# Masked graph attention with eight heads: the output projection takes two heads in one matmul, from data that DMAs move

## The chip, the cores and the metric

The kernel runs on one core of a Trainium2 chip. A core has TensorE (PE, matmuls; its weight loads are told apart as PEld), VectorE (DVE), ScalarE (ACT), GpSimd (POOL) and SyncE (SP), which issues the DMAs here. The metric is the time of one execution on the device in microseconds.

## The reference

Eight graphs (b) of 1024 nodes with 64 features each; adj is an integer matrix of 1024 x 1024 per graph in which about 8 of 1024 entries of a row are not zero. All in float32:

```
h = max(layernorm(x), 0)
q, k, v = h @ Wq + bq, h @ Wk + bk, h @ Wv + bv          # 8 heads of 64
scores = leaky_relu(q . k / 8 + edge_bias[adj], 0.2)     # per head, 1024 x 1024
attn = softmax(where(adj > 0, scores, -1e9))
x + (attn @ v, heads side by side) @ Wp + bp
```

## The kernel before

**Folded weights.** The start folds the weights: scores come from h and a product of Wq and Wk, and v and Wp are folded per head into a 64 x 64 block W_h, so that the output is the sum over heads of (attention-weighted h) @ W_h. These blocks lie in w_ext, [128, 8, 65]: rows 0 to 63 hold W_h, and row 64 has a one in column 64.

**Sparse keys.** The rows of a graph are cut into 8 tiles of 128 queries, and each tile into 8 groups of 16 queries. For each group the kernel gathers the keys that at least one of its queries is joined to, at most 32 from each block of 128 nodes, 256 slots in all. The eight heads of 16 queries are 128 rows, so scores of a group are 128 x 256. A second branch of the program (dense_programs) serves inputs that break these limits; it doesn't run here.

**Steps.** All engines run the same sequence of steps written out in Python. Step s does pair p = s - SCORE of the scores, while other stages work at other lags of the table at line 43 ff.: a stage of lag L treats pair s - L. A pair is two groups; a tile is 4 pairs, so 4 steps; a graph is 32 steps, and there are 32 + 256 steps. `tile(b, s, L)` is true once per tile, `piece(b, s, L, n)` in n steps per tile. Each engine does its share of a step in a fixed order, and semaphores tie them.

A tile runs through: adj_in loaded (LOAD, SP), made bf16 (CONV, POOL), transposed (TURN_A, PE, then ACT), counted (COUNT, PE), ranked, one-hot matrices made (mark, DVE L1670), the masks gathered (MASK, PE L1199, copied to mask_own by ACT L1423), the keys gathered (TFILL, PE L1187, ACT L1432). Then per pair: scores (PE L1164 and L1165, float32r), take_scores (DVE L1658, adds the mask and takes the maximum), the leaky line (POOL L1034), their maximum (DVE L1681), transposes (turn_y, PE L1175), exp (ACT L1441), weigh (PE L1222: probabilities times h and a column of ones, so that row 64 of its result is the sum of the probabilities), copy_o (ACT L1449) to ot_sb, [65, 2, 8, 128], by tile parity.

**Masks.** The masks are made with 16 queries x 8 groups in the rows, but the scores want each query's mask in 8 rows, one per head. move_masks (SP, lag MASK_OUT = 14) stores a tile's masks in DRAM (one DMA of 512 KB), waits until it has landed, and reads them back eight times (mask_rows, eight DMAs of 64 KB). take_scores of that tile's first pair (lag 17) waits for all eight.

**The end of a tile.** project (PE L1253, lags PROJ = 27 and 28) runs twice per tile, with e = 0 and 1, for four heads each: one float32 matmul per head with ot_sb[0:65] of the head as weights (128 columns) and w_ext[0:65] streamed (65 columns), into adj_bank. Column 64 of each result is the sum of the probabilities. A float32 matmul shows in the trace as two pairs of LDWEIGHTS and MATMUL. norm (DVE, lags NORM = 28 and 29) clamps the sums, takes reciprocals, and multiplies; in its first call it also adds the mean of v to rows without any neighbour (`alone`). add_heads (POOL, SUM = 30) adds the eight heads and the residual. SP stores four tiles at once (OUT = 31) and then loads the rows of x for the next graph (x_res). adj_bank is shared with turn_adj and count (PE), whose waits `free` works out: turn_adj (s mod 4 = 1) follows project's second call (s mod 4 = 0) and waits for norm's product of it.

**SP's queue.** SP executes its waits and DMA issues in program order: in a step load_adj, load_stack, move_masks, load_natural, the store of the output. In the start-up, store_graph(k), which stores two forms of a graph's h in DRAM, comes after the steps 0, 2, ... up to 14.

**w_sum** (DVE, s = 18) is the sum of W_h over heads, in both halves of the rows; one matmul per graph (L1329) multiplies the mean of h with it.

## Time and profile before

| what | value |
|---|---|
| median of 3 runs | 1035.78 us (1034.2 to 1037.22) |
| the profiled execution's own time | 1032.86 us |
| its span, first to last instruction | 1030.6 us |
| PE busy | 95% of the span |
| PEld busy | 94% |
| DVE busy | 89% |
| ACT busy | 75% |
| POOL busy | 47% |
| DMA | 125.20 MB in 190760 packets, q1 40.9% of 16 engines |

The busy shares are of the whole span, start-up and end included. A PE matmul's duration is the time from its start to its modelled end, and neighbours overlap, so the cost of one is the distance to the next. "Idle before" is time in which an engine did nothing just before an instruction, with what ended it; "issue" means nothing that the profile shows.

### The profile page before, as it was taken

To read this page: it belongs to the slowest core of one execution; us is meant where nothing else is said; L and a number is where in the kernel's file an instruction comes from. 1 tells how busy PE (TensorE), PEld (TensorE's weight loads), DVE (VectorE), ACT (ScalarE), POOL (GpSimd) and SP (SyncE) were. 2 spreads that over 40 slices of the span, in tenths; PEclk is the share of its full clock that TensorE was granted. 3 is DMA by queue.
4 is the path that set the end of the run, shared out by engine and by line. 5 is a ranking of instruction groups with operands and counts; after the bars stand their busy time and mean duration, and the time that the engine had idled before them with its cause. 6 is when DMAs were issued, how large, how long until landed. Compare 5 with 4: busy or idle time off the path is not lost.

```text
span 1030.6 us, 28703 instructions
## 1 busy us (share of the span) xinstructions
PE 978.6 (95%) x9056; PEld 965.4 (94%) x9056; DVE 914.2 (89%) x3409; ACT 776.0 (75%) x1737; POOL 487.2 (47%) x865
## 2 busy tenths in 40 slices
PE   4578999999999999999999999999999999999996
PEld 4468999999999999999999999999999999999995
DVE  3878899889998999898998899989998899989984
ACT  3587787788778787887777777878777887788762
POOL 1004455455545454554554455545454545555454
PEclk9989999999999999999999999999999999999998
DMA  7574534344343444434343343435343344433220
GB/s 175 184 227 122 145 107 131 104 114 136 113 133 114 121 127 116 134 104 143 103 130 108 113 145 101 137 103 151 104 137 103 109 132 121 135 113 109 77 70 9
DMA packets 190760, 125.20 MB, mean 121 GB/s; under 512 B 32832, under 2 KB 180300, under 8 KB 190604
## 3 DMA queue, kind: packets, MB, share of 16 engines
q1 hardware_dynamic: 189812, 122.75, 40.9%
q8 instruction: 78, 1.28, 0.5%
q10 hardware_dynamic: 792, 0.53, 0.3%
q14 instruction: 78, 0.64, 0.2%
HBM read 79.19 MB, written 44.04 MB: 120 GB/s over the span
## 4 chain that ended last, share of the span: by engine, by line
PE 84%; DVE 9%; issue 2%; DMA 1%; ACT 1%; POOL 1%; SPq 0%; ACTq 0%; POOLq 0%; DVEq 0%
PE bank L1222 20%; PE bank L1253 11%; PE bank L1175 10%; PE bank L1210 8%; PE bank L1164 6%; PE bank L1312 6%; PE bank L1165 5%; PE bank L1187 5%; PE bank L1199 5%; PE bank L1230 3%; DVE w L1658 2%; PE bank L1238 1%; DVE w L1681 1%; DVE o_all L1757 1%; PE bank L1298 1%
## 5 line engine op out<-in xcount | busy, mean ns | idle before, releaser
L1034 POOL TENSOR_SCALAR a_line<-w,a_bias 128x256 f32<-128x256 f32 x512 | 263.3, 514 | 453.3 <-DVE w L1681 411.3
L1222 PE MATMUL bank<-pt,nat_sb 128*65 128x128 f32 x2048 | 265.4, 273 | 0.2
L1658 DVE CUSTOM_DVE_ANT_0 w<-bank,mask_rows 128x256 f32<-128x256 f32 x512 | 195.9, 418 | 60.9 <-issue 56.8
L1441 ACT ACTIVATE pt<-bank 128x512 f32<-128x512 f32 x256 | 153.9, 601 | 110.9 <-PE bank L1175 105.9
L1681 DVE SCALAR_TENSOR_TENSOR w<-w,shift,a_line 128x256 f32<-128x256 f32 x512 | 229.9, 488 | 2.5 <-POOL a_line L1034 2.5
L1222 PEld LDWEIGHTS bank<-pt,nat_sb 128*65 128x65 f32 x2048 | 230.7, 138 | 0.6 <-issue 0.6
L1670 DVE TENSOR_TENSOR onehot<-val,counts_to 128x512 fp32r<-128x512 f32 x256 | 181.1, 707 | 2.2
L1423 ACT ACTIVATE mask_own<-bank,mask_bias 128x512 bf16<-128x512 f32 x256 | 175.1, 684 | 1.1 <-PE bank L1199 1.1
L1175 PE MATMUL bank<-ident,w 128*128 128x128 f32 x1024 | 154.0, 273 | 0.0
L1432 ACT ACTIVATE t_sb<-bank 128x512 fp32r<-128x512 f32 x256 | 150.2, 587 | 2.7 <-PE bank L1187 2.6
L1164 PE MATMUL bank<-t_sb,q_hi 128*128 128x256 f32 x512 | 142.8, 301 | 1.1 <-DVE wmax L1658 1.0
L1253 PE MATMUL bank<-w_ext,ot_sb 65*128 65x65 f32 x1024 | 138.9, 279 | 3.8 <-DVE o_all L1757 3.0
L1449 ACT ACTIVATE ot_sb<-bank 65x256 f32<-65x256 f32 x256 | 97.9, 383 | 55.7 <-PE bank L1222 55.7
L1210 PEld LDWEIGHTS bank<-both_halves,t_sb 128*128 128x128 f32 x1024 | 136.5, 191 | 0.0
L1210 PE MATMUL bank<-both_halves,t_sb 128*128 128x64 f32 x1024 | 136.0, 256 | 0.0
L1468 ACT ACTIVATE q_hi<-bank,q_bias 128x256 fp32r<-128x256 f32 x256 | 107.5, 476 | 36.0 <-PE bank L1312 36.0
L1165 PE MATMUL bank<-t_sb,q_lo 128*128 128x256 f32 x512 | 133.6, 283 | 0.0
L1022 POOL TENSOR_TENSOR o_all<-o_all 128x256 f32<-128x256 f32 (+2 forms) x192 | 120.8, 629 | 21.6 <-DVE o_all L1757 6.6
L1253 PEld LDWEIGHTS bank<-w_ext,ot_sb 65*128 65x128 f32 x1024 | 124.8, 192 | 4.6 <-issue 2.9
L1187 PE MATMUL bank<-onehot,h_nl 128*128 128x256 f32 x512 | 124.1, 324 | 0.4 <-ACT t_sb L1432 0.4
L1632 DVE SCALAR_TENSOR_TENSOR q_lo<-bank,q_bias,q_hi 128x256 fp32r<-128x256 f32 x256 | 111.3, 475 | 9.1 <-ACT q_hi L1468 6.0
L1175 PEld LDWEIGHTS bank<-ident,w 128*128 128x128 f32 x1024 | 118.9, 141 | 0.1
(135 smaller groups left out, 1619.5 us busy)
## 6 DMA issues: line engine op xcount, KB each, us to landing
adj_in<-in_adj_dram SPq DMA_DIRECT2D x64, 512.0 KB, 4.0
mask_store<-mask_own SPq DMA_DIRECT2D x64, 512.0 KB, 3.5
mask_rows<-mask_store SPq DMA_DIRECT2D x512, 64.0 KB, 2.4
nl_store<-nl_ring SPq DMA_DIRECT2D x7, 512.0 KB, 4.1
stack_store<-stage SPq DMA_DIRECT2D x7, 512.0 KB, 2.9
h_stack<-stack_store SPq DMA_DIRECT2D x7, 512.0 KB, 4.5
h_nl<-nl_store SPq DMA_DIRECT2D x28, 128.0 KB, 3.6
x_res<-in_x_dram SPq DMA_DIRECT2D x16, 128.0 KB, 2.3
```

Source lines behind the costliest of these rows:

```text
L1034: nc.gpsimd.tensor_scalar(a_line[:, i % 2, :], w[:, i, :], 5.0, a_bias[:, i:i + 1], ALU.mult, ALU.add)\
L1164: pe.matmul(dst, q_hi[:, y % 2, GPT * (t % 2) + g, :], keys, start=True, stop=False)
L1165: last = pe.matmul(dst, q_lo[:, y % 2, GPT * (t % 2) + g, :], keys, start=False, stop=True)
L1175: last = pe.transpose(turned_bank[:, P * (2 * u + k):P * (2 * u + k) + P], w[:, slot(p, u), P * k:P * k + P], ident[:, :])
L1187: last = pe.matmul(t_bank[:, 256 * i:256 * i + 256], h_nl[:, 2 * f + i, :], onehot[:, t % 2, 2 * f + i].rearrange("p g j -> p (g j)"), sta ...
L1210: last = pe.matmul(nat_bank[:, D * (2 * u + k):D * (2 * u + k) + D], keys[:, P * k:P * k + P], both_halves[:, :], start=True, stop=True)
L1222: last = pe.matmul(o_part[0:D + 1, P * u:P * u + P], nat_sb[:, t % 2, p % 4 * 2 + u, k, :], pt[:, p % 2, u, k, :], start=(k == 0), stop=(k ...
L1253: last = pe.matmul(adj_bank[:, (D + 1) * h:(D + 1) * h + D + 1], ot_sb[0:D + 1, t % 2, 4 * e + h, :], w_ext[0:D + 1, 4 * e + h, :], start= ...
L1423: nc.scalar.activation(mask_own[:, t % 2].rearrange("p g t j -> p t g j")[:, 2 * f:2 * f + 2], m_bank[:, :].rearrange("p (t g j) -> p t g ...
L1658: nc.vector.tensor_tensor_reduce(w[:, i, :], row_bank[:, SLOTS * u:SLOTS * u + SLOTS], mask_rows[:, t % 2, p % 4 * 2 + u, :], 0.25, LEAST_ ...
L1670: nc.vector.tensor_tensor(onehot[:, t % 2, 2 * f:2 * f + 2].rearrange("p t g j -> p (t g) j"), val[:, t % 2, cols * f:cols * f + cols].uns ...
L1681: nc.vector.scalar_tensor_tensor(w[:, i, :], w[:, i, :], shift[:, i:i + 1], a_line[:, i % 2, :], ALU.add, ALU.max).then_inc(y_ready, 1)
```

## The change

- project takes two heads at once. w_pair, [128, 4, 128], holds for heads 2c and 2c + 1 their blocks W on the diagonal: rows 0 to 63 and columns 0 to 63 for the first, the other halves for the second, zeros elsewhere. o_pairs, [128, 2, 4, 128], holds the two heads' results one under the other. A call issues two float32 matmuls of 128 rows, 128 columns of weights and 128 columns streamed.
- The second head of a pair has to move from rows 0 to 63 to rows 64 to 127. move_o on SP (lag MOVE_O = 26) does this with one DMA for each of the two halves (64 rows, 4 pieces of 512 B each), and a third one brings row 64, the sums of 8 heads, into 8 rows (den_rows). Project's first call of a tile turns these with one more float32 matmul (8 rows of weights, 128 columns, against the 8 x 8 identity).
- norm's first call clamps and inverts all eight sums, its second only multiplies. `summed` is waited for just before x_res is written.
- PROJ, NORM, SUM and OUT go from 27, 28, 30, 31 to 31, 32, 34, 35.
- move_masks is split: store_masks in step lag 14, behind move_o in SP's order, spread_masks in step lag 15.
- w_sum has two halves of rows from the two diagonal blocks, and the matmul with the mean of h adds them (two matmuls).
- count and convert get one wait more each (adj_ready, a_turned). COUNT and TURN_A keep their lags 6 and 5.

```diff
-    SCORE, A_LINE, Y, TURN, PV, X_ADD, PROJ, NORM, SUM, OUT = 17, 19, 20, 21, 22, 24, 27, 28, 30, 31
+    MASK, MASK_OUT, MASK_IN, TFILL, QFILL, BETA, COLSUM, VEC = 10, 14, 15, 13, 9, 6, 18, 22
+    SCORE, A_LINE, Y, TURN, PV, X_ADD, MOVE_O, PROJ, NORM, SUM, OUT = 17, 19, 20, 21, 22, 24, 26, 31, 32, 34, 35
...
-            def move_masks(b, t):
+            def store_masks(b, t):
...
                 sp.dma_start(whole, mask_own[:, par].rearrange("p g t j -> p g (t j)")).then_inc(mask_stored[par], 16)
+
+            def spread_masks(b, t):
+
...
                 sp.wait_ge(mask_stored[par], 16 * before + 16)
                 for h in range(H):
                     sp.dma_start(mask_rows[GQ * h:GQ * h + GQ, par], own).then_inc(mask_in[par], 16)
+
+            def move_o(b, t):
+
+                n, par = TPG * b + t, t % 2
+                sp.wait_ge(o_copied, 4 * n + 4)
+                if later(n, 2):
+                    sp.wait_ge(proj_done, 2 * n - 2)
+                heads = o_turned[0:D, par].rearrange("p (c a) q -> p c a q", a=2)
+                for a, rows in enumerate((slice(0, D), slice(D, P))):
+                    sp.dma_start(o_pairs[rows, par], heads[:, :, a]).then_inc(o_moved[par], 16)
+                sp.dma_start(den_rows[0:H, par], o_turned[D:D + 1, par]).then_inc(o_moved[par], 16)
...
+                t = tile(b, s, MOVE_O)
+                if t is not None:
+                    move_o(b, t)
                 t = tile(b, s, MASK_OUT)
                 if t is not None:
-                    move_masks(b, t)
+                    store_masks(b, t)
+                t = tile(b, s, MASK_IN)
+                if t is not None:
+                    spread_masks(b, t)
...
             def project(b, t, e, s):
                 n = TPG * b + t
-                pe.wait_ge(o_copied, 4 * n + 4)
-                free(adj_bank_uses, b, s, len(list(adj_bank_uses(b, s))) - 1)
-                for h in range(4):
-                    last = pe.matmul(adj_bank[:, (D + 1) * h:(D + 1) * h + D + 1], ot_sb[0:D + 1, t % 2, 4 * e + h, :],
-                                     w_ext[0:D + 1, 4 * e + h, :], start=True, stop=True)
+                pe.wait_ge(o_moved[t % 2], 48 * (n // 2) + 48)
+                free(adj_bank_uses, b, s, 0)
+                for c in range(2):
+                    last = pe.matmul(adj_bank[:, P * c:P * c + P], o_pairs[:, t % 2, 2 * e + c, :], w_pair[:, 2 * e + c, :],
+                                     start=True, stop=True)
+                if e == 0:
+                    last = pe.matmul(adj_bank[:, 2 * P:2 * P + H], den_rows[0:H, t % 2, :], ident[0:H, 0:H],
+                                     start=True, stop=True)
                 last.then_inc(proj_done, 1)
...
-                    pe.matmul(misc[:, 0:D], mean_rep[:, :], w_sum[:, :], start=True, stop=True).then_inc(vec_done, 1)
+                    for a in range(2):
+                        last = pe.matmul(misc[:, 0:D], mean_rep[:, :], w_sum[:, a, :], start=(a == 0), stop=(a == 1))
+                    last.then_inc(vec_done, 1)
...
                 if i == 0 and later(TPG * b + t, 2):
-                    act.wait_ge(proj_done, 2 * (TPG * b + t) - 2)
+                    act.wait_ge(o_moved[t % 2], 48 * ((TPG * b + t) // 2))
...
             def norm(b, t, e):
                 n, heads = TPG * b + t, slice(4 * e, 4 * e + 4)
                 dve.wait_ge(proj_done, 2 * n + e + 1)
-                if e == 0 and later(n):
-                    dve.wait_ge(summed, n)
-                parts = adj_bank[:, 0:4 * (D + 1)].rearrange("p (h d) -> p h d", d=D + 1)
-                nc.vector.tensor_scalar(den[:, heads], parts[:, :, D], 1e-30, None, ALU.max).then_inc(den_ready, 1)
+                parts = adj_bank[:, 0:2 * P].rearrange("p (h d) -> p h d", d=D)
                 if e == 0:
...
+                    sums = adj_bank[:, 2 * P:2 * P + H]
+                    nc.vector.tensor_scalar(den[:, :], sums, 1e-30, None, ALU.max).then_inc(den_ready, 1)
+                    nc.vector.tensor_scalar(alone[:, :], sums[:, 0:1], 0.5, None, ALU.is_lt).then_inc(alone_ready, 1)
+                    dve.wait_ge(den_ready, n + 1)
+                    nc.vector.reciprocal(den_inv[:, :], den[:, :]).then_inc(den_inv_ready, 1)
...
+                    if later(n):
+                        dve.wait_ge(summed, n)
...
-                nc.vector.tensor_tensor(o_all[:, heads, :], parts[:, :, 0:D],
-                                        den_inv[:, heads].unsqueeze(2).to_broadcast([P, 4, D]), ALU.mult)\
+                    dve.wait_ge(den_inv_ready, n + 1)
+                nc.vector.tensor_tensor(o_all[:, heads, :], parts, den_inv[:, heads].unsqueeze(2).to_broadcast([P, 4, D]), ALU.mult)\
                     .then_inc(proj_taken, 1)
```

## Rows read from the trace of the kernel before

**Rows 1.** The page: span, then busy us, share of the span, instructions.
```profile
span 1030.6 us, 28703 instructions
...
PE 978.6 (95%) x9056; PEld 965.4 (94%) x9056; DVE 914.2 (89%) x3409; ACT 776.0 (75%) x1737; POOL 487.2 (47%) x865
```
**Rows 2.** The page: the chain that ended last, shares of the span by engine.
```profile
PE 84%; DVE 9%; issue 2%; DMA 1%; ACT 1%; POOL 1%; SPq 0%; ACTq 0%; POOLq 0%; DVEq 0%
```
**Rows 3.** Busy us (instructions) per engine in three stretches, PE clock, DMA share, GB/s.
```profile
150.00:950.00 800.00, 792.94 (x7478) 787.16 (x7477) 736.03 (x2789) 628.90 (x1415) 407.78 (x714) 1.00 0.42 121
501.30:530.70 29.40, 28.31 (x263) 27.97 (x262) 28.66 (x101) 21.77 (x49) 15.21 (x27) 1.00 0.41 115
...
440.00:469.40 29.40, 29.29 (x279) 29.08 (x278) 26.30 (x103) 23.22 (x53) 15.50 (x27) 1.00 0.35 97
```
**Rows 4.** The chain in order of time, 716 to 720: start us, us, what.
```profile
716.60 0.92 PE bank L1253 x8
...
718.05 0.12 PE bank L1164
...
718.53 0.44 PE bank L1175 x4
718.97 0.87 PE bank L1222 x8
```
**Rows 5.** Groups by form: project's weight loads, busy us, mean ns, idle.
```profile
L1253 PEld LDWEIGHTS bank<-w_ext,ot_sb 65*128 65x128 f32 x1024 | 124.8, 192 | 4.6 <-issue 2.9 <-ACT ot_sb L1449 1.5
```
**Rows 6.** Timeline of DVE, the second norm of a tile: start us, us, what.
```profile
738.08 0.15 DVE L1742 TENSOR_SCALAR den<-bank 128x4 f32<-128x4 f32 x1
...
738.49 0.42 DVE L1757 TENSOR_TENSOR o_all<-bank,den_inv 128x256 f32<-128x256 f32 x1
```
**Rows 7.** Waits from 150 to 950 us: us in total, times, longest.
```profile
PEld bank L1230 <- issue: 8.7, 33, 0.5
```
**Rows 8.** Timeline of ACT, SP and DVE around two moves of masks.
```profile
499.64 0.38 ACT L1449 ACTIVATE ot_sb<-bank 65x256 f32<-65x256 f32 x1 [0.28 <-PE bank L1222]
...
501.10 0.38 SPq L904 DMA_DIRECT2D mask_store<-mask_own  x1
...
505.81 3.63 SPq L909 DMA_DIRECT2D mask_rows<-mask_store  x8
...
514.23 0.41 DVE L1658 CUSTOM_DVE_ANT_0 w<-bank,mask_rows 128x256 f32<-128x256 f32 x1
...
848.75 3.64 SPq L909 DMA_DIRECT2D mask_rows<-mask_store  x8
...
855.86 0.41 DVE L1658 CUSTOM_DVE_ANT_0 w<-bank,mask_rows 128x256 f32<-128x256 f32 x1
```
**Rows 9.** The page: DMA issues, KB each, median us from issue to landing.
```profile
mask_store<-mask_own SPq DMA_DIRECT2D x64, 512.0 KB, 3.5
mask_rows<-mask_store SPq DMA_DIRECT2D x512, 64.0 KB, 2.4
```
**Rows 10.** Timeline of the start-up: ACT, SP and DVE.
```profile
66.86 0.60 ACT L1377 ACTIVATE stage<-bank 128x512 fp32r<-128x512 f32 x1 [0.20 <-PE bank L1105]
...
67.30 3.67 SPq L909 DMA_DIRECT2D mask_rows<-mask_store  x8
...
71.01 0.43 SPq L947 DMA_DIRECT2D nl_store<-nl_ring  x1
...
72.97 0.42 DVE L1658 CUSTOM_DVE_ANT_0 w<-bank,mask_rows 128x256 f32<-128x256 f32 x1 [0.87 <-DMA mask_rows<-mask_store]
```
**Rows 11.** Timeline of the end: PE, DVE and SP.
```profile
1019.46 1.11 PE L1253 MATMUL bank<-w_ext,ot_sb 65*128 65x65 f32 x8 [0.47 <-ACT ot_sb L1449]
...
1021.21 0.16 DVE L1742 TENSOR_SCALAR den<-bank 128x4 f32<-128x4 f32 x1 [2.23 <-POOL x_res L1025]
...
1026.67 0.40 SPq L893 DMA_DIRECT2D out_dram<-x_res  x1
```

More of the change, by code:

```diff
@@ L80, in preln_graph_attention @@
         w = sb("w", [P, 2 * RING, SLOTS], F32, fast)
-        ot_sb = sb("ot_sb", [P, 2, H, P], F32, fast)
+        o_turned = sb("o_turned", [P, 2, H, P], F32, fast)
         pt = sb("pt", [P, 2, 2, 2, P], F32, fast)
@@ L258, in preln_graph_attention @@
         o_copied = sem("o_copied")
+        o_moved = [sem(f"o_moved{i}") for i in range(2)]
         proj_done = sem("proj_done")
@@ L666, in dense_scalar @@
                 for rows in (slice(0, D), slice(D, P)):
-                    nc.scalar.activation(vp_hi[rows, :].rearrange("p (h d) -> p h d", h=H), w_ext[0:D, :, 0:D],
-                                         ACT.Copy).then_inc(v_weights, 1)
+                    for a, heads in enumerate((slice(0, D), slice(D, P))):
+                        last = nc.scalar.activation(vp_hi[rows, :].rearrange("p (c a d) -> p a c d", a=2, d=D)[:, a],
+                                                    w_pair[heads, :, D * a:D * a + D], ACT.Copy)
+                    last.then_inc(v_weights, 1)
                 def q_hi_parts(b, k):
@@ L738, in dense_vector @@
                 for rows in (slice(0, D), slice(D, P)):
-                    nc.vector.tensor_tensor(vp_lo[rows, :].rearrange("p (h d) -> p h d", h=H), w_ext[0:D, :, 0:D],
-                                            vp_hi[rows, :].rearrange("p (h d) -> p h d", h=H).bitcast(F32), ALU.subtract)\
-                        .then_inc(v_weights, 1)
+                    for a, heads in enumerate((slice(0, D), slice(D, P))):
+                        lo, hi = (part[at, :].rearrange("p (c a d) -> p a c d", a=2, d=D)[:, a]
+                                  for part, at in ((vp_lo, rows), (vp_hi, heads)))
+                        last = nc.vector.tensor_tensor(lo, w_pair[heads, :, D * a:D * a + D], hi.bitcast(F32), ALU.subtract)
+                    last.then_inc(v_weights, 1)
                 def add_beta(g):
@@ L904, in move_masks @@
                 sp.dma_start(whole, mask_own[:, par].rearrange("p g t j -> p g (t j)")).then_inc(mask_stored[par], 16)
+            def spread_masks(b, t):
+                par, before = t % 2, MT * b + t // 2
+                own = mask_store[par].rearrange("(g r s) -> r g s", r=P + GQ, s=SLOTS)[0:GQ]
                 if later(before):
@@ L1404, in _ @@
                                          ACT.Copy, scale=QSCALE).then_inc(hi_weights, 1)
-                nc.scalar.activation(w_ext[0:D].rearrange("p (c a) d -> p a c d", a=2)[:, a, :, 0:D],
+                nc.scalar.activation(w_pair[both[a], :, D * a:D * a + D],
                                      second[0:D, 0:256].rearrange("p (c d) -> p c d", d=D), ACT.Copy)\
@@ L1796, in _ @@
                 if s == 18:
-                    for rows in both:
-                        last = nc.vector.tensor_reduce(w_sum[rows, :], w_ext[0:D, :, 0:D].rearrange("p h d -> p d h"), AX_X, ALU.add)
+                    for a, heads in enumerate(both):
+                        for rows in both:
+                            last = nc.vector.tensor_reduce(w_sum[rows, a, :], w_pair[heads, :, D * a:D * a + D]
+                                                           .rearrange("p c d -> p d c"), AX_X, ALU.add)
                     last.then_inc(w_sum_ready, 1)
```

27 lines of the change are left out of this document (11 added, 16 removed).

## The prediction

> **What bounds the kernel now.** I read the engines' totals first: TensorE (PE) is busy 978.6 of 1030.6 us, VectorE (DVE) 914.2 [rows 1]. A busy PE need not be what sets the end, so the chain of work that ended last comes next: 84% of the span lies on PE, 9% on DVE [rows 2]. Then single stretches. From 150 to 950 us PE is busy 792.94 of 800 us at the full granted clock of 1.00, DVE 736.03 [rows 3]. So in the steady part PE's own instruction stream is the bound. One place is close to changing hands: of 29.4 us (two tiles of 128 queries, eight steps), DVE is busy 26.30 in an ordinary stretch and 28.66 in the stretch in which the edge biases of the next graph are worked out, where PE is down to 28.31 [rows 3]. There the two are level.
>
> What a PE instruction costs is read from the distances on the chain, not from its duration, since matmuls overlap. A float32 matmul is two pairs of weight load and matmul in the trace. One call of project (4 heads, 8 pairs, weights of 128 columns, 65 columns streamed) takes 0.92 us, 0.115 a pair; weigh streams 128 columns against 65 columns of weights in 0.87 us, 0.109 a pair; a step of scores (128 columns of weights, 256 streamed in fp32r) takes 0.12 a pair; a transpose with 128 columns of weights and 128 streamed 0.11 [rows 4]. So project is bound by its weight loads: a load of 128 columns lasts 192 ns [rows 5], and since one starts every 0.115 us, loads overlap what runs before them.
>
> **1. Two heads in one matmul.** project issues 2 matmuls (4 pairs) where it issued 4 (8 pairs). Each new pair loads 128 columns and streams 128: the load at most 0.115 apart (project now), the streaming 0.109 (weigh). If they overlap as they do in scores, the larger of both decides: 0.115 to 0.12; I take 0.12, the row with both sides full. 4 x 0.12 = 0.48 against 0.92: 0.44 saved, of which I keep 0.43 for the change-over to the next group. Bounds: 4 x 0.109 saves 0.48; if load and matmul don't overlap (0.115 + 0.109 = 0.224 a pair) 4 x 0.224 = 0.90 and 0.02 is saved. 128 calls x 0.43 = 55.0 us less on PE.
>
> By the Trainium skill ("TensorE: Matmul & The Clock Gate", Back-to-back issue gap) a sustained stream of load and matmul at 128 columns goes at about 81 ns a pair. The float32 rows here show 0.109 to 0.115 at the full clock, so I keep those; by the page's figure the four pairs would take about 0.32 us and 128 calls would save 20 us more. The same page (Part 3, The mechanism) says that weight loads overlap running matmuls only when the row groups differ, which speaks against this change: its matmuls fill all 128 rows. The rows of scores, full in rows and columns, stand against it (0.12 a pair, loads of 0.19 us).
>
> **2. The sums of exp in a matmul of their own.** One more float32 matmul per tile: 2 pairs, 8 rows, 8 columns streamed, but 128 columns of weights each. The load decides, at project's distance: 2 x 0.115 = 0.23 us, 64 x 0.23 = 14.7 us. Upper bound: two full pairs and an uncovered change-over, 0.33; lower bound: two at weigh's distance, 0.22; if few rows made a load cheaper, down to 0, for which no row speaks. With part 1 PE gains 2 x 0.43 - 0.23 = 0.63 us per tile.
>
> **3. w_sum in two halves.** 8 more float32 matmuls in all, 16 pairs x 0.115 = 1.8 us more. PE so far: -55.0 + 14.7 + 1.8 = -38.5 us. The four DVE reductions of 4 heads for two of 8 lie in the start-up, the same elements: nothing, at most 0.5 us.
>
> **4. norm.** The clamp and the reciprocal are done once per tile for 8 heads instead of twice for 4. In the second call the product followed them by a chain of self-waits: from the clamp's start to the product's start 738.08 to 738.49, 0.41 us [rows 6]. That goes, and the first call gets 4 elements longer: DVE gains 0.41 us per tile, nothing on PE's path where PE is the bound. It matters for what is late next: PE's transposes of the adjacency wait for that product (8.7 us of idle on this line in 33 waits from 150 to 950 us) [rows 7]. PE comes to them 0.43 us earlier after the first call's norm, DVE's product 0.41 earlier: this wait stays as it is. The wait for `summed` moves behind the clamp; POOL's additions keep their distance (SUM and NORM both move by four).
>
> **5. Four steps later.** PROJ, NORM, SUM and OUT move by 4, so they keep their place among the four steps of a tile, next to the same work on PE, DVE and POOL. In the steady part that costs nothing: a tile's 4 steps shift its output, not its rate. x_res is loaded 4 steps later, but its first use (X_ADD) is still 9 steps off, over 30 us. At the end it costs, see 8.
>
> **6. The moves on SyncE's queue.** Three DMAs per tile, in front of the tile's store of masks. o_turned is ready at 500.02, while the store waits for the mask copies and goes out at 501.10. An issue takes some 0.43 us (8 of them 3.63, the store 0.38): the three end at about 501.35, the store is 0.25 us later [rows 8]. Their 520 packets (512 B) run on the same 16 engines. Nearest row: a 64 KB spread lands in 2.4 us, a 512 KB store in 3.5 [rows 9], so 256 KB more in front of a store are worth (3.5 - 2.4) / 448 x 256 = 0.6 us, from 0 (through before the store starts) to 2.4 (one whole landing). The data themselves are needed five steps (18 us) later: hidden with 15 us to spare. Behind them on SP: store, spreads, adj_in. The spreads begin 505.81, the last goes out near 509.0 and lands near 511.4; the first reader is DVE's take_scores at 514.23 [rows 8]: 2.8 us of cover. It loses 0.25 + 0.6 and the 0.6 by which PE's tile gets shorter, which leaves about 1.3. Where the store lands late it is just used up: spreads from 848.75, so the last landing near 854.3, reader at 855.86, 1.5 of cover [rows 8]. I take 1 us in all, bounds 0 and, with the store held by 2.4, 0.5 us on each of 64 tiles, 30 us.
>
> **7. Store and spreads in two steps.** The spreads keep their waits; in the loop only load_natural's first piece and nothing of length comes between. In the start-up it is not so: after step 14 SP runs store_graph(7), which waits for the last graph's copies, and now stands in front of tile 0's spreads. They went out at 67.30, before its stores at 71.01; DVE already waits 0.87 us for them at 72.97. The last copy of that graph ends at 67.46 [rows 10], so the spreads go out near 68 and behind 1 MB of stores: 1 to 2.5 us later. Part of it has cover, since DVE's later steps are not yet full: I take 1 us once, 0 to 2.5.
>
> **8. The end.** Now the last tile's project starts at 1019.46, right after its copy, DVE's clamp waits for POOL until 1021.21, and the last store goes out at 1026.67 [rows 11]. After: that copy is followed by three issues and a landing (about 0.9 + 2.3), project starts near 1022.6; meanwhile tile 6's two projections, norm and additions run. Then project 0.7, norm 1.1 behind tile 6's additions, project 0.5, product 0.4, additions 2.1: the store near 1028.7, 2.0 later. Two projections leave the stretch before, which PE bounded; 0.8 us of that is beyond what part 1 counted. Net +1.2 us, 0 to 3.
>
> **9. Where DVE takes over.** In the stretch at 501.3 DVE is busy 28.66 of 29.4 and loses 2 x 0.41, which with its short self-waits is about 28.4; PE wants 29.4 - 2 x 0.63 = 28.1. The gain there is 0.5 us smaller, once per graph: 4 us. In ordinary stretches DVE needs 26.30 - 0.82 = 25.5 of 28.1: PE stays the bound.
>
> Sum: -38.5 + 4 (part 9) + 1 (6) + 1 (7) + 1.2 (8) = -31.3, say -30. The profiled execution took 1032.86 us with its span of 1030.6; it would come to about 1003. The median of the timed runs is 1035.78, 2.9 above it, so I forecast 1006. Less than 0.3% (3 us) can't be told from no change.
>
> **Rivals.** (a) DVE becomes the bound more widely, through coupling: PE's next scores wait for take_scores, PE's transposes for the product. For it: 92% busy, the level stretch. Against it: 64 us idle in 800. If every tile hands back a third of a microsecond, 64 x 0.33 = 21 of the 30 are lost but for part of the 4 counted: 1006 + 17 = 1023 at worst, 1016 in the middle. Chance 0.12.
> (b) The masks are late: the moves hold the store longer than the 1.3 us of cover. Each further 1 us costs up to 1 us per tile, since PE's transposes stand behind take_scores and the product. With 0.2 to 0.4 us per tile 1019 to 1031; it decides to the other side from 0.47 per tile (30 / 64). Chance 0.08, of which 0.02 slower.
> (c) Slower than before: weight load and matmul of a full float32 pair don't overlap. Place: project. Price 0.224 a pair: parts 1 to 3 become -128 x 0.02 + 14.7 + 1.8 = +14, with 7 and 8 +16: 1052. It turns where 128 x (0.92 - 4p) pays for 14.7 + 1.8 + 2.2, at p = 0.19. For it: no row has a plain float32 pair with both sides full; against it: scores at 0.12, transposes at 0.11. Chance 0.06.
> (d) The pair is faster, 0.081, also in the extra matmul: 20 + 4 us more, 982; DVE would take part of it, about 988. Against it every float32 row. Chance 0.01.
>
> **How the numbers follow.** Main case 0.73, its own range 998 to 1014 (38.5 with nothing lost; 22 with a pair at 0.135 and DVE a little more in the way). With most of (a) and the light side of (b) the range is 998 to 1021, which leaves out the worst of (a) and (b), (c) and (d): under 0.2. Faster by over 0.3%: 0.90; within: 0.02; slower: 0.08.
>
> **What would show it.** Right: the four pairs of a project at 0.46 to 0.48 us on the chain, the pair for the sums 0.23, PE still at 98 to 99% of the steady stretches, a tile 0.55 to 0.6 us shorter than now, the reader of the masks seldom waiting for DMA, and the last 10 us about 1 us longer. Wrong: PE idle of tenths of a microsecond per tile before scores or the transposes (a); waits of DVE's take_scores that end with the landing of mask_rows (b); pairs at 0.2 (c).

## The result and the profile after

The changed kernel takes 1027.43 us (median of 6 runs, 1025.0 to 1028.77) against 1034.3 us (6 runs, 1033.1 to 1037.22) of the kernel before in the same comparison: ratio 0.9924 [0.9905, 0.9943]. It is faster, by 7 us and not by the 30 that I forecast; 1027 is outside my range. The profiled execution's span is 1026.3 us, for which my sum gave about 1000 (1030.6 less 30).

The page after, its engine totals, then 150 to 950 us (before: [rows 3]; busy us and instructions of PE, PEld, DVE, ACT, POOL, then PE clock, DMA share, GB/s):

```profile
span 1026.3 us, 28211 instructions
...
PE 972.7 (95%) x8688; PEld 941.7 (92%) x8688; DVE 885.7 (86%) x3283; ACT 774.3 (75%) x1737; POOL 489.6 (48%) x864
...
150.00:950.00 800.00, 793.34 (x7253) 772.32 (x7252) 718.92 (x2715) 634.44 (x1430) 414.75 (x722) 1.00 0.51 140
```

Against [rows 1, 3]: PE has 368 matmuls less and looks just as full, 99% of the stretch, at the same granted clock. DVE is busy 17.1 us less in 800 us, in which it now gets through more tiles; per tile that is 0.46 us less (13.66 to 13.20), where part 4 gave 0.41. By busy shares nothing is wrong. A PE row's duration covers its modelled end, though, so a matmul that starts late still leaves the engine "busy" through the one ahead. The distance from one matmul's start to the next one's doesn't hide that. I took it for the 48 tiles between the 25th and the 217th call of scores, before and after (ns per tile; a wait is counted with the group that stands ahead of it):

| group | before | after | | forecast |
|---|---|---|---|---|
| project, two calls (L1253, L1281) | 1813 | 1350 | -463 | -860 |
| matmul of the sums (L1284) | 0 | 317 | +317 | +230 |
| rank (L1245, L1273) | 30 | 134 | +104 | 0 |
| gap ahead of the transposes of adjacency | 388 | 180 | -208 | 0 |
| other waits in that group, w_sum, the rest | | | +80 | +28 |
| whole tile | 14846 | 14676 | -170 | -602 |

The 400 ns by which project misses its forecast have three main parts. The forecast leaves 953 for eight pairs, 119 each. The first pair of each call lasts 191 ns from start to start, where it was 139: 145 too much for the two calls, of which the four inner pairs, at 112, give back 28. The step from project's last matmul to the first of the sums is 205, 86 too much. The distance from the last matmul of the second call to the rank matmul is 316: 204 of it is a wait, as shown below.

48 tiles give 8.2 us. In the profiled executions, outside these tiles, the time from the last scores to the end grew from 24.3 to 26.9 us, the last 40 steps by 1.2, the start to the 25th scores by 0.1: 1030.6 - 8.2 + 2.7 + 1.2 + 0.1 = 1026.3 us with rounding.

PE from project of the first half to the fill of q (timeline: start us, us, what):

```profile
503.88 0.69 PE L1281 MATMUL bank<-w_pair,o_pairs 128*128 128x128 f32 x4
504.50 0.38 PE L1284 MATMUL bank<-ident,den_rows 8*128 8x8 f32 x2
504.83 0.39 PE L1343 MATMUL bank<-h_stack,g_hi 128*128 128x256 f32 x1
505.06 0.28 PE L1343 MATMUL bank<-h_stack,g_lo 128*128 128x256 f32 x1
```

The four matmuls of L1281 start at 503.875, 504.068, 504.179 and 504.291: but for the first, which takes 0.19, the pairs are 0.11 apart, so load and matmul of a full float32 pair do overlap, as part 1 has it. The 0.19 stands in every kernel with the new project (0.189 to 0.192 in the mean), whether it waited or not; no run shows its cause. But the first matmul with 8 rows of weights starts 0.205 us behind the last with 128 rows, in every one of the 48 tiles, and the next full one 0.18 behind the second small one, where before the step to the fill of q took 0.083.

VectorE, GpSimd and TensorE in the step of the second half's project, the worst of its kind:

```profile
507.22 0.20 DVE L1778 RECIPROCAL den_inv<-den 128x8 f32<-128x8 f32 x1
507.30 1.05 POOL L1038 TENSOR_SCALAR adj_bf<-adj_in 128x1024 bf16<-128x1024 int32 x1
507.34 1.08 DVE L1786 SCALAR_TENSOR_TENSOR x_res<-vecs,alone,x_res 128x64 f32<-128x64 f32 x1
...
508.34 0.41 DVE L1790 TENSOR_TENSOR o_all<-bank,den_inv 128x256 f32<-128x256 f32 x1
508.67 0.86 DVE L1665 SCALAR_TENSOR_TENSOR q_lo<-bank,q_bias,q_hi 128x256 fp32r<-128x256 f32 x2
...
508.89 0.68 PE L1281 MATMUL bank<-w_pair,o_pairs 128*128 128x128 f32 x4 [0.69 <-DVE o_all L1790]
...
509.65 0.10 PEld L1273 LDWEIGHTS bank<-used,lower 128*128 128x128 bf16 x1 [0.26 <-issue]
```

VectorE adds to x_res (64 columns, 0.25 us elsewhere) from 507.34 to 508.42, just as long as GpSimd's conversion of adjacency runs. Its product, the free bank and project come that much later. Then the rank matmul waits for q_lo, which frees its bank: q_lo ends at 509.53, the load starts at 509.65. In all 48 tiles the rank matmul starts 0.145 to 0.147 us after q_lo's end, so q_lo is what releases it. On average it starts 0.316 us after the last one of project, where it was 0.112 before.

Waits from 150 to 950 us (in total, times, longest), which answer to [rows 7]:

```profile
DVE q_lo L1665 <- ACT q_hi L1501: 13.2, 47, 0.3
PEld bank L1273 <- issue: 8.8, 39, 0.3
PEld bank L1257 <- issue: 2.5, 7, 0.8
...
DVE w L1691 <- DMA mask_rows<-mask_store: 1.6, 3, 0.9
```

As much as stood ahead of the transposes of adjacency (8.7 us) now stands ahead of the rank matmul (8.8), and 2.5 are left ahead of the transposes. SyncE's queue around a move of masks, which answers to [rows 8]:

```profile
496.63 1.29 SPq L930 DMA_DIRECT2D o_pairs<-o_turned  x2
497.96 0.71 SPq L931 DMA_DIRECT2D den_rows<-o_turned  x1
498.78 0.38 SPq L910 DMA_DIRECT2D mask_store<-mask_own  x1
502.04 4.93 SPq L920 DMA_DIRECT2D mask_rows<-mask_store  x8
```

Start-up (answers to [rows 10]) and end ([rows 11]), from the timeline and from the chain that ended last:

```profile
67.30 4.35 SPq L920 DMA_DIRECT2D mask_rows<-mask_store  x8
...
74.08 0.42 DVE L1691 CUSTOM_DVE_ANT_0 w<-bank,mask_rows 128x256 f32<-128x256 f32 x1 [3.38 <-DMA mask_rows<-mask_store]
```
```profile
1010.13 1.07 PE bank L1249 x8
1011.22 0.39 ACT o_turned L1482
1011.63 0.62 SPq L930
1012.29 0.62 SPq L930
1012.95 2.02 DMA den_rows<-o_turned
1015.01 1.23 PE bank L1281 x4
1016.24 0.54 PE bank L1284 x2
```

Stretches at the end (columns as above: PE, PEld, DVE, ACT, POOL, PE clock, DMA share, GB/s):

```profile
1010.00:1015.00 5.00, 2.52 (x19) 2.16 (x18) 1.88 (x7) 0.38 (x1) 2.12 (x5) 0.92 0.28 57
1015.00:1016.80 1.80, 1.75 (x6) 1.43 (x6) 0.00 (x1) 0.00 (x0) 1.52 (x4) 0.50 0.00 0
```

PE had been idle half of the five us before, and then its clock is 0.50, the lower level (1.2 GHz). The last tile's two projections run at that clock, 1.23 and 1.21 us on the chain; before the change only its second one met a lower clock (0.75 in the mean of 1022.0 to 1023.7).

### The profile page after: what moved, and what is told of

Read it like the earlier page. It is cut to its first block and busy times, and to the rows that moved or that the text cites. A ratio compares the mean times of both kernels' runs of the same rounds, so it can differ in the third digit from the quotient of the medians.

```text
span 1026.3 us, 28211 instructions
## 1 busy us (share of the span) xinstructions
PE 972.7 (95%) x8688; PEld 941.7 (92%) x8688; DVE 885.7 (86%) x3283; ACT 774.3 (75%) x1737; POOL 489.6 (48%) x864
## 3 DMA queue, kind: packets, MB, share of 16 engines
q8 instruction: 75, 1.23, 0.5%
## 5 line engine op out<-in xcount | busy, mean ns | idle before, releaser
L1703 DVE TENSOR_TENSOR onehot<-val,counts_to 128x512 fp32r<-128x512 f32 x256 | 178.1, 696 | 2.2
L1465 ACT ACTIVATE t_sb<-bank 128x512 fp32r<-128x512 f32 x256 | 152.3, 595 | 4.0 <-PE bank L1214 3.9
L1482 ACT ACTIVATE o_turned<-bank 65x256 f32<-65x256 f32 x256 | 99.3, 388 | 56.0 <-PE bank L1249 56.0
L1226 PE MATMUL bank<-onehot,adj_t 128*128 128x256 f32 x512 | 105.0, 287 | 0.9 <-ACT mask_own L1456 0.5
L1191 PEld LDWEIGHTS bank<-t_sb,q_hi 128*128 128x128 f32 x512 | 97.3, 190 | 6.8 <-DVE wmax L1691 3.4
```

What stands on the lines that cost most here:

```text
L1191: pe.matmul(dst, q_hi[:, y % 2, GPT * (t % 2) + g, :], keys, start=True, stop=False)
L1465: nc.scalar.activation(t_sb[:, t % 2].rearrange("p g t j -> p t g j")[:, 2 * f:2 * f + 2], t_bank[:, :].rearrange("p (t g j) -> p t g j", ...
L1703: nc.vector.tensor_tensor(onehot[:, t % 2, 2 * f:2 * f + 2].rearrange("p t g j -> p (t g) j"), val[:, t % 2, cols * f:cols * f + cols].uns ...
```

## The experiments

A tile takes four steps. I name them by what they hold: **A** project of the first half, the sums and the fill of q; **B** project of the second half and rank; **C** the transposes of adjacency; **D** the counts. VectorE's chain runs from B to C: scores taken, division and product of the first half, q_lo, the next scores, product of the second half. Only then is the bank free for the transposes. PE's step lengths (us, start of scores to start of scores, means over the same 48 tiles), the start-to-start gap ahead of the transposes, VectorE's addition to x_res, and the time against the kernel before in the same job:

| kernel | B | C | D | A | tile | gap | x_res | us | ratio [95%] |
|---|---|---|---|---|---|---|---|---|---|
| before | 3.621 | 3.958 | 3.124 | 4.143 | 14.846 | 0.388 | 0.340 | | |
| after | 3.570 | 3.761 | 3.150 | 4.194 | 14.676 | 0.180 | 0.375 | 1027.4 | 0.992 [0.991, 0.994] |
| e1 128 rows for the sums | 3.684 | 3.851 | 3.151 | 3.963 | 14.650 | 0.273 | 0.502 | 1023.4 | 0.988 [0.986, 0.991] |
| e2 no sums | 3.728 | 3.836 | 3.153 | 3.803 | 14.519 | 0.257 | 0.545 | 1017.0 | 0.982 [0.980, 0.984] |
| e3 rank later | 3.302 | 3.961 | 3.151 | 4.191 | 14.605 | 0.262 | 0.421 | 1021.9 | 0.987 [0.986, 0.989] |
| e4 masks in one step | 3.585 | 3.784 | 3.149 | 4.189 | 14.708 | 0.202 | 0.396 | 1024.7 | 0.990 [0.988, 0.992] |
| e5 = e1 + e3 | 3.321 | 4.031 | 3.151 | 3.963 | 14.466 | 0.337 | 0.449 | 1012.7 | 0.979 [0.978, 0.980] |
| e7 conversion at 3 | 3.468 | 3.734 | 3.150 | 4.196 | 14.548 | 0.151 | 0.272 | 1023.1 | 0.990 [0.989, 0.992] |
| e8 x_res in second half | 3.404 | 3.810 | 3.150 | 4.199 | 14.563 | 0.230 | 0.275 | 1020.1 | 0.986 [0.985, 0.988] |
| e10 all | 3.228 | 3.917 | 3.150 | 4.002 | 14.297 | 0.222 | 0.276 | 1001.9 | 0.970 [0.968, 0.971] |
| e11 before + e7 + e8 | 3.585 | 3.836 | 3.124 | 4.167 | 14.713 | 0.267 | 0.275 | 1027.5 | 0.994 [0.993, 0.995] |
| e12 store first | 3.529 | 3.736 | 3.150 | 4.193 | 14.608 | 0.153 | 0.340 | 1021.0 | 0.988 [0.987, 0.990] |
| e13 all, conversion at 4 | 3.133 | 3.931 | 3.150 | 3.977 | 14.191 | 0.240 | 0.276 | 995.8 | 0.963 [0.962, 0.965] |
| e14 all, conversion at 2 | 3.174 | 3.915 | 3.149 | 4.137 | 14.375 | 0.223 | 0.275 | 1006.1 | 0.973 [0.972, 0.975] |

The median of the kernel before was 1035.0 us in the job of e1 to e4, 1034.3 in that of e5 to e10 (and of the changed kernel), 1033.5 in that of e11 to e14. Gains below are differences of medians to the 1027.4 us of the changed kernel, so they hold to 1 or 2 us: by the ratios e7 gains 2.4 us and not 4.3, e12 4.2 and not 6.4, e8 6.3, e5 13.9, e13 30. The columns of a tile come from one execution, which can lie 3 us from its kernel's median (e7 3.0 below, e4 2.4 above), 0.05 us per tile; less than that tells nothing.

One more split of the same 48 tiles is needed below. VectorE's addition to x_res takes about 0.25 us in some tiles and much longer in others. PE's step B, and in it the start-to-start distance ahead of project's second call, for tiles with an addition under 0.3 us and for the rest:

| kernel | tiles with a long addition | B, short | B, long | ahead of project, short | long |
|---|---|---|---|---|---|
| after | 20 | 3.461 | 3.724 | 0.112 | 0.297 |
| e1 | 31 | 3.425 | 3.826 | 0.112 | 0.407 |
| e3 | 27 | 3.153 | 3.417 | 0.112 | 0.311 |
| e5 | 26 | 3.135 | 3.478 | 0.112 | 0.390 |

PE waits there only in tiles with a long addition.

### e1: the sums' matmul with 128 rows

```diff
-                    last = pe.matmul(..., den_rows[0:H, t % 2, :], ident[0:H, 0:H],
+                    last = pe.matmul(..., den_rows[:, t % 2, :], ident[:, 0:H],   # den_rows set to 0 once
```

> The changed kernel, but the matmul for the sums of exp takes 128 rows of weights (rows 8 to 127 are zeros, set once) instead of 8. Same columns, same two pairs. Then here both gaps go, the call with e = 0 gets 0.25 to 0.3 us shorter, and 64 tiles give 15 to 18 us: 1010 to 1013 us. Rival T: the extra matmul costs what it costs by its two weight loads and a third group in the bank, whatever its rows: 1027 us, same gaps. Rival D: PE gets shorter but DVE holds it, waits of the same size appear elsewhere: 1022 to 1027 with the gaps gone.

The matmul itself (timeline of e1):

```profile
503.98 0.69 PE L1282 MATMUL bank<-w_pair,o_pairs 128*128 128x128 f32 x4
504.51 0.29 PE L1285 MATMUL bank<-ident,den_rows 128*128 128x8 f32 x2
504.80 0.38 PE L1344 MATMUL bank<-h_stack,g_hi 128*128 128x256 f32 x1
```

From the last matmul of project to the sums' first takes 0.112 us in every tile, not 0.205, the second small matmul follows the first by 0.031, not 0.133, and the fill of q follows it by 0.112 in the median, not 0.181. Step A is 0.23 us shorter with more rows of weights: the cost is the change of shape, not the load. But B grew by 0.11 and C by 0.09, and the tile kept 0.03. B's 0.11 stands ahead of project's second call, which waits for the product of the first half: the addition to x_res ahead of that product was long in 31 of 48 tiles instead of 20. In the tiles with a short one B didn't grow (3.425 against 3.461). So the gaps went as theory S has it, and the time stayed in the range of rival D. By the Trainium skill ("TensorEngine Tiling (Array Packing)", Key Properties) a change of the tiling mode drains TensorE, and a mode with 32 rows is one of those it lists; the two gaps agree with that, on entry and on leaving, though no row shows in what mode a matmul ran.

### e2: no matmul of the sums

```diff
-                if e == 0:
-                    last = pe.matmul(adj_bank[:, 2 * P:2 * P + H], den_rows[0:H, t % 2, :], ...)
```

The division then uses what happens to stand in the bank; the output is not the reference's.

> The changed kernel without the matmul for the sums of exp (its result is left out; norm reads what lies in the bank). Theory S: the matmul costs 0.5 us per tile with its two drains, 64 x 0.5 = 32 us: 995 to 1000 us, the rest lost to DVE. If it costs only its two loads (0.23 us), 15 us: 1012 us. If DVE is the bound after the change, under 8 us: 1019 to 1027 us.

Step A is 0.39 us shorter, so the whole extra matmul, with the gaps around it, costs that much; B and C give back 0.23. The 1017.0 us lie between the 1012 of the plain loads and the 1019 to 1027 of VectorE as the bound: of 25 us in PE's stream (64 x 0.39) 10 come off.

### e3: rank behind the weighing, one step later

```diff
-    LOAD, CONV, COUNT, TURN_A, USED, RANK, ... = 0, 4, 6, 5, 7, 8, ...
+    LOAD, CONV, COUNT, TURN_A, USED, RANK, ... = 0, 4, 6, 5, 7, 9, ...
         weigh(b, p)
+        rank(b, t, s)      # was behind project
```

> The changed kernel, but PE does the ranking matmul one step later, after weigh, so that it no longer follows project's second call at once. Theory W: in the changed kernel PE stands still for about 0.2 us per tile before the ranking matmul (0.32 us after project's last matmul instead of 0.11), because that matmul's bank is freed by DVE's q_lo, which DVE reaches after the norm; PE used to come later. It isn't shown as idle time since the last matmul's modelled end covers it. Then the gap goes here, 0.15 to 0.2 us per tile, of which the wait before the adjacency transposes takes some back: 1016 to 1022 us. Rival: the 0.32 us is a cost of PE after a full float32 matmul, then it follows project to whatever comes next, and the time is 1027 us.

Theory W holds: the 0.32 us don't stay behind project (0.147 to the next scores), and the rank matmul follows weigh at 0.109. B loses 0.27 us. C gains 0.20, of which 0.11 is the rank matmul itself, which now stands there, and 0.08 the longer wait ahead of the transposes. 1021.9 us is at the upper end of what I expected.

### e4: store and spreads of masks in one step again

```diff
-    MASK, MASK_OUT, MASK_IN, ... = 10, 14, 15, ...
+    MASK, MASK_OUT, MASK_IN, ... = 10, 14, 14, ...
```

> The changed kernel with store and spreads of masks in one step of SyncE again (MASK_IN = 14). My reading: the split costs only in the start-up, where store_graph(7) stands in front of tile 0's spreads; undone, the first takes of scores start 1 to 2.5 us earlier: 1025 to 1026.5 us. Rival: the split also matters in the loop (a load of the natural rows goes out between): then 3 us or more, either way.

1024.7 us is 2.7 us less, but the runs overlap (1023.4 to 1027.1 against 1025.0 to 1028.8), so a gain isn't shown. The first reading of masks comes 0.7 us earlier (73.38 against 74.08), and at the 25th call of scores nothing is left of it (156.9 against 157.0). The profiled execution is 1.0 us shorter, 1.6 longer in the 48 tiles (14.708 against 14.676) and 2.2 shorter in the last 40 steps (135.7 us against 137.9). The reading that the split costs 1 to 2.5 us in the start-up isn't borne out.

### e5: e1 and e3 together

> Both single changes at once: the sums' matmul with 128 rows of weights (zeros below the eight sums) and the rank matmul behind the weighing one step later. Alone they gave 1023.4 and 1021.9 us against 1027.4 us of the changed kernel. Theory S (the drains and the rank's wait are costs of TensorE's own stream): the two gains of 4.0 and 5.5 us stand in different steps, phase 3 and phase 0 of the four steps of a tile, and add up: about 1018 us. Theory D (VectorE's chain through phases 0 and 1 holds TensorE, which sits in whichever wait is left): phase 0 and phase 1 together give back what is taken from phase 3: no better than the better of the two, 1020 to 1023 us, with the wait ahead of the transposes of adjacency above 0.3 us per tile.

1012.7 us: 14.7 us below the changed kernel, where the single changes gave 4.0 and 5.6. I had expected the sum at best. A loses its 0.23 as in e1, B its 0.25 as in e3, and only C gives back, 0.27, of which 0.11 is the rank matmul in its new place. In e1 alone B took back 0.11, ahead of project. The split by additions says where the difference lies: in tiles with a short addition B is 3.461, 3.425, 3.153 and 3.135 in after, e1, e3 and e5, so there the gains just add up, and what differs is how often the addition is long: 11 tiles more in e1 than in the changed kernel, one less in e5 than in e3. Another 2.4 us come off before the 25th scores (157.0 to 154.6), where e1 lost 0.9. So the excess over the sum is no proof that two waits hide each other's removal; what makes the addition long is the next experiment's question.

### e7: GpSimd's conversion one step earlier; e8: the addition to x_res behind the second half's product

```diff
-    LOAD, CONV, COUNT, ... = 0, 4, 6, ...
+    LOAD, CONV, COUNT, ... = 0, 3, 6, ...          # e7
```
```diff
                 if e == 0:
                     ...
-                    nc.vector.scalar_tensor_tensor(x_res[...], vecs[...], alone[:, :], x_res[...], ...)
                 nc.vector.tensor_tensor(o_all[:, heads, :], parts, den_inv[...], ALU.mult)
+                if e == 1:
+                    nc.vector.scalar_tensor_tensor(x_res[...], vecs[...], alone[:, :], x_res[...], ...)   # e8
```

> Only GpSimd's conversion of adjacency moves, one step earlier, so that it no longer runs in the step in which VectorE adds the vector to x_res. If VectorE's addition is stretched because GpSimd's conversion runs beside it (theory C), the addition is 0.26 us again in nearly every tile (after: 0.30 us mean, 12 of 64 over 0.5 us) and the kernel gains at most 48 x 0.04 = 2 us, and the conversion stretches something of VectorE in phase 3 instead. If the stretch has another cause (theory N), the long ones stay, and the time stays 1027 us.

> VectorE's addition to x_res moves from the first half's division (phase 0) to behind the second half's product (phase 1). Theory D (VectorE's chain from the scores of phase 0 to the transposes of adjacency is what ends last): the chain is 0.3 us shorter, per tile 0.1 to 0.3 us comes off phases 0 and 1, 1013 to 1022 us. Theory T (TensorE's own stream and single waits set the time): the wait ahead of the transposes falls but nothing else, at most 0.1 us per tile, 1023 to 1028 us.

Groups from 150 to 950 us (busy us, mean ns), first e7, then e8:

```profile
L1714 DVE SCALAR_TENSOR_TENSOR w<-w,shift,a_line 128x256 f32<-128x256 f32 x440 | 228.1, 558 | 0.0
...
L1038 POOL TENSOR_SCALAR adj_bf<-adj_in 128x1024 bf16<-128x1024 int32 x55 | 80.8, 1468 | 4.6
L1786 DVE SCALAR_TENSOR_TENSOR x_res<-vecs,alone,x_res 128x64 f32<-128x64 f32 x55 | 14.9, 270 | 0.0
```
```profile
L1714 DVE SCALAR_TENSOR_TENSOR w<-w,shift,a_line 128x256 f32<-128x256 f32 x440 | 197.0, 488 | 0.0
L1038 POOL TENSOR_SCALAR adj_bf<-adj_in 128x1024 bf16<-128x1024 int32 x55 | 57.6, 1047 | 4.6
L1792 DVE SCALAR_TENSOR_TENSOR x_res<-vecs,alone,x_res 128x64 f32<-128x64 f32 x55 | 15.1, 275 | 0.0
```

Theory C holds: the addition follows GpSimd's place. In e7 it is short again (11 of 48 over 0.5 us in the changed kernel, one in e7), and now one addition of the scores meets the conversion in 36 of the 48 tiles and takes about 1.25 us: the mean of all of them goes from 488 to 558 ns. The conversion goes from 1047 to 1468, also in tiles in which no such addition meets it. More time is lost to the meeting in e7, but it lies where VectorE isn't late, and 4.3 us come off (2.4 by the ratios). My bound of 2 us was worked out from a wrong mean: the addition takes 0.375 us in the 48 tiles of the changed kernel and 0.353 in all 64, not 0.30, so the stretch is 0.10 us per tile, 5 us in 48. e8 takes 0.17 us off B and gives back 0.05 in C: 7.4 us, theory D.

### e10, e13, e14: all at once, the conversion in three places

> All at once: 128 rows for the sums, rank one step later, the store of masks ahead of the moves of o with the loads one step earlier, the conversion one step earlier, the addition to x_res in the second half. Theory D: with VectorE's chain shortened, the gains of the matmul stream are no longer given back: 1005 to 1013 us. Theory T: the gains stay partly given back as in the single changes, 1015 to 1020 us.

> All changes of the 1001.9 us kernel but the conversion back in its old step, where VectorE no longer has the addition to x_res beside it. The earlier step stretched VectorE's additions of the scores instead (0.488 to 0.558 us, 48 of 256 over 0.6 us). If that collision costs (theory C), 995 to 1001 us; if the old step's collision with the rest of the division costs more, 1002 to 1007 us.

> The same with the conversion two steps earlier than in the changed kernel, in the step of GpSimd's own sums over heads. If only the meeting with VectorE's long instructions counts, 995 to 1001 us; if GpSimd's own work in that step delays the lines of the scores, VectorE waits for them, 1003 to 1010 us.

e10's 1001.9 us lie below even theory D's 1005 to 1013; e13 and e14 lie in the ranges of theory C and of GpSimd's own work. e13 is the best version: 995.8 us, 3.7% under the kernel before and 31.6 us under the changed one. Its 150 to 950 us:

```profile
150.00:950.00 800.00, 796.28 (x7488) 789.76 (x7488) 753.58 (x2807) 660.82 (x1479) 432.36 (x746) 1.00 0.52 143
```

PE works off 235 matmuls more than the changed kernel in the same 800 us. With x_res gone from its side no addition is stretched in step B any more (0.276 us for that to x_res, 0.491 for those of the scores). One step earlier the conversion costs 6 us (e10, where 36 additions of the scores take over 0.6 us in the 48 tiles), two steps earlier 10 (e14, where 84 do, and A is 0.15 us longer ahead of the fill of q, which my expectation laid to the lines of the scores). How e14's 10 us divide isn't shown. The gap ahead of the transposes is 0.240 us still, so VectorE's chain is not free even there.

### e11: the same relief on the kernel before

> The kernel before with only the two edits that shorten VectorE's chain: the conversion one step earlier and the addition to x_res behind the second half's product. On the changed kernel they gave 4.3 us and 7.4 us alone. Theory D (the same chain already held TensorE in the kernel before: its transposes of adjacency waited 0.39 - 0.12 = 0.27 us per tile): 10 to 17 us less, 1018 to 1025 us, and that wait falls under 0.2 us. Theory E (the chain holds TensorE only since the change made its stream shorter): 1030 to 1035 us.

6.0 us and 0.133 us per tile, between the two theories. So the chain held PE already before the change, but by less than its wait ahead of the transposes seemed to offer: that gap only fell from 0.388 to 0.267. The wait should have fallen under 0.2 us, and it didn't. To see what the change is worth once this chain is shorter, e10 is the one to set beside e11, since both have the conversion at 3: 14.713 to 14.297, 0.42 us per tile, and 25.2 us in the span (1025.2 to 1000.0). With the conversion at 4, which e11 doesn't have, e13 is 0.52 us and 30.4 us below e11. Both also hold e1, e3, e12's order and the masks in one step, so that they come near what I forecast for the change alone (0.60 and 30) doesn't bear the forecast out.

### e12: the store of masks ahead of the moves

```diff
-                if t is not None: move_o(b, t)       # tile at MOVE_O
                 ... store_masks(b, t)
+                if t is not None: move_o(b, t)
```

> Only SyncE's order within a step changes: the store of masks goes ahead of the three moves of o, so it no longer waits for their issues (1.29 + 0.71 us in the changed kernel). If these issues are what makes the masks late (part 6), the slack from the last mask landing to the first reading of scores is 1 to 1.5 us longer, the six to eight tiles that waited wait no longer (7.6 us of waits in all), and 2 to 5 us come off: 1022 to 1025 us. If the masks are late for the transfers themselves, 1026 to 1028 us.

SyncE's queue in e12:

```profile
496.07 0.38 SPq L910 DMA_DIRECT2D mask_store<-mask_own  x1
496.55 1.76 SPq L930 DMA_DIRECT2D o_pairs<-o_turned  x2
498.36 0.71 SPq L931 DMA_DIRECT2D den_rows<-o_turned  x1
499.55 4.44 SPq L920 DMA_DIRECT2D mask_rows<-mask_store  x8
```

6.4 us (4.2 by the ratios), more than the 2 to 5 that I had expected. From the last mask's landing to its first reader the median is 2.6 us again (2.7 before, 1.8 after), and the waits of scores on these transfers fall from 7.6 to 2.8 us in the whole run. What is left is the first tile's wait in the start-up (3.4 in the changed kernel); the 1.6 us from 150 to 950 and the 2.6 near the end are gone. In the profiled executions 3.3 us come off in the 48 tiles and 3.3 in the last 40 steps, so these waits cover 4.2 of 6.6 us; no run takes the rest apart (the addition to x_res is also shorter, 0.375 to 0.340).

## Why the prediction was wrong

**Direction and part 1's mechanism held.** A full float32 pair costs 0.11 us, rivals (c) and (d) are out. What failed in part 1 is the price of the call, "4 x 0.12 = 0.48 against 0.92": its first pair takes 0.19, so the call in step A is 0.42 us to its last matmul and then stands 0.21 ahead of the 8-row one (0.62 in all); in step B it is followed by the rank's wait, 0.32 (0.73). The calls save 0.27 and 0.19 us instead of 0.43. In e1, with no change of shape behind it, the call in step A takes 0.53.

**Part 2's price was mis-sized too.** I took 0.23, "the load decides", and no row had told of a change in the number of weight rows. It is 0.39 us (step A, after against e2); with 128 rows it is 0.16 (e1 against e2), so 0.23 of it is the change of shape: from start to start 0.205 against 0.112 on entering, 0.133 against 0.031 between its two matmuls and 0.181 against 0.112 on leaving (medians). Nor did the load decide in one shape: in e1 the two pairs start 0.031 apart, though each loads 128 columns. "If few rows made a load cheaper" was a bound that looked only down; few rows made it dearer.

**Part 4's sentence "this wait stays as it is" failed.** VectorE did lose its time (0.46 us per tile), and the wait ahead of the transposes did not stay: it fell by 0.21 us, and came back ahead of the rank matmul (0.20) and behind it (0.10). I had followed one wait of the chain, the one that the list of waits showed, and not the chain itself. That is rival (a), coupling, given 0.12. Of the 0.43 us per tile that is missing, about 0.3 lies in PE's own stream (first pairs, change of shape, the sums) and about 0.13 in waits for VectorE: rank 0.20 and 0.10, project's second call 0.03, less the 0.21 ahead of the transposes. But the two don't simply add, and this is what the sum left out: a PE stream that is 0.23 us shorter (e1) left the tile 0.03 shorter (0.06 by the 4.0 us of its time), and 0.39 (e2) left it 0.16 shorter, while moving one addition off VectorE's chain (e8) gave 0.11 without touching PE. With e1 and e3 in PE's stream the tile is 14.466 (e5), and with the addition moved and the masks stored first as well 14.191 (e13).

**Part 9 looked for the wrong sign of it.** I compared busy sums, 26.3 of 29.4 us. A chain through two steps held PE (e8, e11) while VectorE was idle a tenth of the time elsewhere. Nor did I ask what VectorE's instructions meet on GpSimd: the addition to x_res, long in 20 of 48 tiles, is what PE waits for ahead of project's second call.

**Part 6** had the mechanism, but the issues last 0.62 to 0.71 us, not 0.43, and the three come ahead of the store in full: 1.1 us later instead of 0.25. e12 puts it at 4 to 6 us against 1 forecast; rival (b) in part.

**Part 7**: the first reading is 1.1 us later (74.08 against 72.97), but not by the path given: the spreads start at 67.30 as before and take 4.35 us to issue. And the delay doesn't last: the 25th call of scores is 0.1 us later, against 1 forecast. **Part 8**: 2.7 us against 1.2; the sums' matmul (0.54) stands on the path, and both last projections run at the lower clock (1.23 and 1.21 us, for which I had 0.7 and 0.5). **Parts 3 and 5** held: 28 ns per tile for w_sum, the steps in their places.

Sum per tile: forecast -0.60; project +0.40, sums +0.09, rank +0.10, transposes -0.21 and small ones +0.05 lead to -0.17.

## What to carry to other kernels

When a shortened engine stands in a ring with another, add up the other engine's chain from the point where it gets its input to the point where it frees the bank, wait by wait, before crediting the saving: busy shares, and the one wait that the list names, don't show it. Read starts of matmuls, not busy time. Before saying where a gain went, split the tiles by the instruction that varies: here one addition, stretched in some tiles and not in others, decided how much of a saving was kept. Keep a stream's weights in one shape: padding 8 rows with zeros to 128 was 0.23 us per tile cheaper in PE's stream than changing to 8, though only 4 us of the 15 came off the time until VectorE's chain was shortened too.

## What was not expected of the hardware

**A short VectorE instruction is held for as long as a GpSimd one runs.** In the changed kernel the addition to x_res takes 0.24 to 0.25 us when it starts ahead of the conversion, and when it starts behind its start it ends 0.05 to 0.15 us after the conversion's end (31 tiles, from 140 us on), wherever it began: 184.56 + 0.52 with the conversion to 185.00, 229.16 + 0.34 with it to 229.43, 272.90 + 1.11 with it to 273.94, 507.34 + 1.08 with it to 508.35. GpSimd's addition of the constant to x_res, once in four tiles, does the same: 214.54 + 0.54 beside 214.27 + 0.73. In e7 two additions of the scores take 1.65 us together for some 0.9: the first, which starts beside the conversion, 1.25, the second 0.47.

```profile
704.56 0.95 DVE L1714 SCALAR_TENSOR_TENSOR w<-w,shift,a_line 128x256 f32<-128x256 f32 x2
706.51 1.46 POOL L1038 TENSOR_SCALAR adj_bf<-adj_in 128x1024 bf16<-128x1024 int32 x1
706.99 1.65 DVE L1714 SCALAR_TENSOR_TENSOR w<-w,shift,a_line 128x256 f32<-128x256 f32 x2
```

The Trainium skill ("SBUF — State Buffer", Who interferes with whom) calls the ports that VectorE and GpSimd share an exclusive lock held for an instruction; these rows agree in that the addition ends only behind the conversion. They don't show one running wholly after the other: what is left behind the conversion's recorded end, 0.07 us in most tiles, is less than the addition's own 0.24. It goes the other way too: in e7 the conversion starts while VectorE makes the one-hot matrices (706.51, within 706.39 + 0.68) and takes 1.46 us for 1.05. Which instructions of VectorE need the ports these runs don't show.

**The change between weights of 128 rows and of 8 costs time both ways**, 0.205 and 0.181 us start to start where full shapes take 0.112. **An issue of a move between two on-chip tensors holds SyncE's queue 0.62 to 0.71 us** in the changed kernel, against 0.38 for the store of 512 KB.

What stays open: why the first pair of a call of the new project takes 0.19 us; how the 0.24 us ahead of the transposes in e13 splits over VectorE's chain; what e1 and e3 give together once the addition to x_res is never stretched, without the other changes of e10; and whether padding costs anything where the stream is bound by something else. None of these was tried.
